# A causal mask as a fourth matmul pass, and a query rounding placed later on ScalarE and VectorE

## The chip, the cores and the metric

One core of a Trainium2 chip runs the whole program. The metric is the device time of one execution in microseconds (us). The kernel before takes 1631.67 us, the median of three runs.

## What is computed

A transformer layer: attention with a mixed key set, a residual and a layer norm, then a feed-forward part with Walsh-Hadamard transforms, a second residual and layer norm. Input is 4 x 1024 x 512 in float32. For the change only the attention's last 256 queries of each sequence matter. Cut to that:

```python
q_geo, k_geo = _rope(q_geo, pos, ROPE_BASE), _rope(k_geo, pos, ROPE_BASE)
remote = Tq - LW                     # 768; the first 768 keys are averaged in blocks of 64
pool = lambda a: concatenate([a[:, :, :remote].reshape(...).mean(axis=3), a[:, :, remote:]], axis=2)
k_pos = concatenate([arange(12) * 64 + 63, arange(768, 1024)])
scores = (q_sem @ k_sem2.T + q_geo @ k_geo2.T) / sqrt(32) * exp(logit_scale)
mask = k_pos[None, :] <= pos[:, None]
scores = where(mask, scores, -1e9)
probs = softmax(scores, axis=-1)
out = probs @ v2                     # 16 heads, 4 key heads
return out @ Wo
```

A query at position 768 or later sees all 12 averaged keys and the last 256 keys up to its own position. A query before 768 sees averaged keys only.

## The kernel before, in words

The program has two blocks, one after the other: `attention_block` (four sequences, called batches; the first three run in a hardware loop, the fourth stands behind it) and `ffn_block`, which the change leaves alone. Each engine runs its own instruction list in order, written out by hand, and waits on semaphores; a `Signal` counts how often a step has been done.

Precision is kept by splitting each float32 operand into a high part, rounded to `float32r`, and a low part, the rest. A product is three passes on TensorE (`three_passes`, lines 92 to 96): high x high, high x low, low x high. The rounding to the high part is ScalarE's (ACT), the subtraction that leaves the low part VectorE's (DVE) or GpSimd's (POOL).

A batch has 8 query tiles of 128 queries. Tiles 0 to 5 see averaged keys only. Tiles 6 and 7 (`tt` = 0 and 1) are the local ones: their scores have 12 + 128 = 140 and 12 + 256 = 268 keys. They are worked off in rounds. A group is one of the 4 key heads of one of the two tiles, so there are 8 groups (0 to 3 of the first tile, 4 to 7 of the second), with 4 query heads each, taken as two pairs. In round i of `ROUNDS` = 10:

- TensorE transposes the probabilities of group i-2 (`local_transposes`, L1098, into tile `mid`), makes the scores of group i (`local_scores`, L94 to L96 into `big`) and multiplies the transposed probabilities of group i-2 with the values (`local_values`, into `tr`). Between them stand the output products (`output`, into `acc`) and, in round 2, the transposes of the second tile's queries (`transpose_queries`, L929).
- VectorE adds the triangular mask to the last 128 keys of each pair of heads in PSUM (L800), takes the row maxima (L802), and later the reciprocals of the sums (L836). It makes low parts: of the transposed probabilities (`tp_lo`, L822), of the attended values (`qo_lo`, L848), and of the transposed queries (L790).
- ScalarE takes the exponentials with their sums (`local_exponentials`, L552), and makes high parts: `tp_hi` (L581), `qo_hi` (L601), and the queries' (`transposed_queries`, L508; the second tile's lie in the memory of `xs_hi` and `xs_lo`).
- GpSimd multiplies the exponentials by the reciprocals (`normalise`, L373 and L374).

The scores of a pair go into `pair_scores(tt, p)`: for the first tile into half a bank for each head (banks 0 and 1 in turn), for the second into a bank for each head (banks 2 and 3, then 0 and 1). So a pair's scores may start only when the exponentials of the pair two before have read theirs. The second tile's transposed queries lie in banks 2 and 3 until both parts are taken. The first scores of the second tile, in round 4, wait for the low part of those queries (`qt_lo_s`).

What TensorE does in round i, shortened:

```python
if i >= 2:
    local_transposes(i - 2)
if 1 <= i < GROUPS:
    local_scores(i)
if i == 2:
    transpose_queries(b, 1)
if i in (4, 8):
    output(b, RT + i // 8, 0)
if i >= 2:
    local_values(i - 2)
```

## Time and profile before

| what | value |
|---|---|
| three runs | 1630.94, 1631.67, 1631.96 us |
| the profiled execution's own time | 1631.06 us |
| its span, first to last instruction | 1628.9 us |
| mean granted TensorE clock, share of full | 0.982 |
| TensorE (PE) busy | 1544.5 us, 95% |
| TensorE weight loads (PEld) busy | 1382.1 us, 85% |
| VectorE (DVE) busy | 1065.5 us, 65% |
| ScalarE (ACT) busy | 617.8 us, 38% |
| GpSimd (POOL) busy | 464.1 us, 28% |

A TensorE row has two parts in this profile: the weight load (PEld) and the matmul (PE). Matmuls are pipelined: the duration of one holds its passage through the array, so what a pass costs is the distance from its start to the next one's. Idle time "before" an instruction is that of its engine, and the name behind the arrow is what released it.

### The profile page before, as it was taken

What the parts mean: (1) busy time and instruction counts of PE and PEld (TensorE: products, weight loads), DVE (VectorE), ACT (ScalarE), POOL (GpSimd) and SP (SyncE); (2) the same over time, 40 slices, a digit from 0 to 9 for tenths busy, and PEclk for the clock granted to TensorE, in tenths of its full rate; (3) what the DMA queues carried; (4) which work ended last, traced back from release to release, by engine and by line L of the source; (5) the groups of instructions that cost most, each with busy time, mean ns of one, the idle gap of its engine ahead of it and who ended that gap; (6) DMA issues with size and microseconds to landing.
All of it is one profiled execution on the core that took longest, in us unless ns stands there. A gap on an engine that the chain in (4) does not pass through costs nothing.

```text
span 1628.9 us, 28725 instructions
## 1 busy us (share of the span) xinstructions
PE 1544.5 (95%) x10152; PEld 1382.1 (85%) x10152; DVE 1065.5 (65%) x1835; ACT 617.8 (38%) x1255; POOL 464.1 (28%) x584
## 2 busy tenths in 40 slices
PE   6989999998998589999999999999999999999997
PEld 5976977887887478889999988999998999999996
DVE  6876777677687488885565565467556557557644
ACT  4253144236225344543343343333333333334322
POOL 5365356437346442330030030040021013003000
PEclk9999999999999889999999999999999999999999
DMA  6031122122211486677767756776867766866861
GB/s 264 17 111 51 33 78 97 35 78 98 68 65 40 167 324 258 246 277 249 263 221 262 272 205 226 277 236 230 309 200 243 280 235 219 287 234 223 284 230 64
DMA packets 92086, 307.72 MB, mean 189 GB/s; under 512 B 9888, under 2 KB 10272, under 8 KB 90144
## 3 DMA queue, kind: packets, MB, share of 16 engines
q1 hardware_dynamic: 90928, 301.54, 52.6%
q10 hardware_dynamic: 1008, 4.20, 0.6%
q8 instruction: 91, 1.49, 0.4%
q14 instruction: 59, 0.48, 0.1%
HBM read 255.37 MB, written 50.33 MB: 188 GB/s over the span
## 4 chain that ended last, share of the span: by engine, by line
PE 60%; DVE 3%; issue 1%; ACT 0%; POOL 0%; DVEq 0%; POOLq 0%; ACTq 0%
PE ff_bank_b L1747 16%; PE ff_bank_a L1747 10%; PE ff_bank_c L1747 10%; PE ff_acc L94 7%; PE ff_acc L96 7%; PE ff_acc L95 7%; DVE ff_d_lo L1561 1%; PE ff_x_ps L1718 1%; PE ff_x_ps L1700 1%; DVE ff_x_lo L1546 1%; DVE ff_ring L1551 0%; PE ff_x_ps L1708 0%; PE ff_x_ps L1709 0%; DVE ff_c L1607 0%; PE ff_acc L1797 0%
## 5 line engine op out<-in xcount | busy, mean ns | idle before, releaser
L1747 PE MATMUL ff_bank_b<-ff_x_hi,ff_ring 128*128 128x256 f32 x1536 | 306.4, 282 | 11.0 <-DVE ff_c L1601 8.0
L1747 PEld LDWEIGHTS ff_bank_b<-ff_x_hi,ff_ring 128*128 128x128 f32 x1536 | 250.7, 190 | 13.2 <-DVE ff_ring L1551 7.7
L1747 PE MATMUL ff_bank_b<-ff_x_lo,ff_ring 128*128 128x256 f32 x768 | 215.9, 281 | 0.0
L1747 PE MATMUL ff_bank_a<-ff_x_hi,ff_ring 128*128 128x256 f32 x1024 | 206.4, 284 | 7.9 <-issue 5.8
L94 PE MATMUL ff_acc<-ff_d_hi,ff_h_hi 128*128 128x512 f32 x512 | 203.8, 398 | 2.7 <-DVE ff_d_lo L1561 2.7
L1747 PE MATMUL ff_bank_c<-ff_x_hi,ff_ring 128*128 128x256 f32 x1024 | 204.9, 283 | 0.0
L96 PE MATMUL ff_acc<-ff_d_hi,ff_h_lo 128*128 128x512 f32 x512 | 199.7, 390 | 0.0
L95 PE MATMUL ff_acc<-ff_d_lo,ff_h_hi 128*128 128x512 f32 x512 | 199.4, 389 | 0.0
L1747 PEld LDWEIGHTS ff_bank_a<-ff_x_hi,ff_ring 128*128 128x128 f32 x1024 | 167.8, 191 | 11.8 <-issue 9.4
L1747 PEld LDWEIGHTS ff_bank_c<-ff_x_hi,ff_ring 128*128 128x128 f32 x1024 | 165.8, 188 | 1.9 <-issue 1.7
L1601 DVE TENSOR_TENSOR ff_c<-ff_bank_b,ff_c 128x512 f32<-128x512 f32 x64 | 44.2, 690 | 174.1 <-PE ff_bank_b L1747 168.9
L1747 PEld LDWEIGHTS ff_bank_b<-ff_x_lo,ff_ring 128*128 128x128 f32 x768 | 145.7, 190 | 0.0
L1747 PE MATMUL ff_bank_a<-ff_x_lo,ff_ring 128*128 128x256 f32 x512 | 144.2, 282 | 0.0
L1747 PE MATMUL ff_bank_c<-ff_x_lo,ff_ring 128*128 128x256 f32 x512 | 143.2, 280 | 0.0
L1452 ACT ACTIVATE ff_sg<-ff_c,h_ug_scale 128x512 f32<-128x512 f32 (+1 forms) x128 | 79.0, 617 | 136.8 <-DVE ff_c L1617 102.3
L94 PEld LDWEIGHTS ff_acc<-ff_d_hi,ff_h_hi 128*128 128x128 f32 x512 | 96.1, 188 | 23.0 <-issue 4.7
L1465 ACT ACTIVATE ff_c<-ff_bank_a 128x512 f32<-128x512 f32 x64 | 38.2, 597 | 202.6 <-PE ff_bank_a L1747 202.6
L96 PEld LDWEIGHTS ff_acc<-ff_d_hi,ff_h_lo 128*128 128x128 f32 x512 | 96.1, 188 | 21.2
L1637 DVE TENSOR_TENSOR ff_h_lo<-ff_hf,ff_h_hi 128x512 fp32r<-128x512 f32 x128 | 101.5, 830 | 18.0 <-ACT ff_h_hi L1494 17.4
L95 PEld LDWEIGHTS ff_acc<-ff_d_lo,ff_h_hi 128*128 128x128 f32 x512 | 96.2, 188 | 20.0 <-issue 1.7
L1747 PEld LDWEIGHTS ff_bank_a<-ff_x_lo,ff_ring 128*128 128x128 f32 x512 | 97.5, 190 | 2.6 <-issue 0.2
L1747 PEld LDWEIGHTS ff_bank_c<-ff_x_lo,ff_ring 128*128 128x128 f32 x512 | 96.2, 188 | 1.9 <-issue 1.9
(303 smaller groups left out, 3416.0 us busy)
## 6 DMA issues: line engine op xcount, KB each, us to landing
ff_ring<-gu_scratch SPq DMA_DIRECT2D x392, 512.0 KB, 4.9
gu_scratch<-ff_ring SPq DMA_DIRECT2D x56, 512.0 KB, 3.9
at_xt<-in_xt SPq DMA_DIRECT2D x4, 2048.0 KB, 8.3
at_xn<-in_x SPq DMA_DIRECT2D x32, 256.0 KB, 2.9
x_scratch<-at_x SPq DMA_DIRECT2D x32, 256.0 KB, 2.0
ff_raw<-in_wgu SPq DMA_DIRECT2D x8, 1024.0 KB, 6.4
at_wd_a<-in_wd SPq DMA_DIRECT2D x8, 512.0 KB, 3.8
mixed_scratch<-at_wd_a SPq DMA_DIRECT2D x8, 512.0 KB, 3.1
```

What stands on the lines that cost most here:

```text
L94: pe.matmul(out, lhs_hi, rhs_hi, start=first, stop=False)
L95: pe.matmul(out, lhs_hi, rhs_lo, start=False, stop=False)
L96: return pe.matmul(out, lhs_lo, rhs_hi, start=False, stop=last)
L1452: return act.activation(target, source, ACT.Silu, scale=ug_scale[:, 1, 2 * p + j:2 * p + j + 1])
L1465: act.activation(c2[:, 0, :, :], bank_a[:, :, :], ACT.Copy).then_inc(m1_s.sem, 1)
L1546: dve.tensor_tensor(x_lo[:, k, :, :], tokens(k), x_hi[:, k, :, :].bitcast(F32), ALU.subtract).then_inc(x_lo_s.sem, 1)
L1561: i = dve.tensor_tensor(by_piece(d_lo[:, j, :]), down_chunk(2 * p + j), by_piece(d_hi[:, j, :]).bitcast(F32), ALU.subtract)
L1601: dve.tensor_tensor(c12[:, :, :], bank_b[:, :, :], c2[:, 0, :, :], ALU.add).then_inc(evict_s.sem, 1)
L1637: dve.tensor_tensor(h_lo[q][:, 1 - j, :], hf[:, 1 - j, :], h_hi[q][:, 1 - j, :].bitcast(F32), ALU.subtract).then_inc(h_lo_s.sem, 1)
L1700: i = pe.transpose(x_ps[:, P * t:P * t + P], y[parity][:, t, P * c:P * c + P], ident[:, :])
L1718: pe.matmul(x_ps[:, :], had[:, :], down_chunk(i), start=True, stop=True).then_inc(w_had, 1)
L1747: i = pe.matmul(bank[:, m, :], r[:, a, m, c, :], b[:, k, c, :], start=(k < 3 and m == 0 and c == 0 and b is x_hi and a == 0), stop=(m == 1 ...
```

## The change

Two things. First, the addition of the mask in PSUM goes from VectorE, and its semaphore `lmasked` with it. In its place TensorE runs a fourth pass between the first and the second of each head's three: the identity (`ident_r`) as the stationary operand, the triangular mask (`causal_r`) as the moving one, 128 columns wide, accumulated into the last 128 keys. Both are `float32r` copies of tables that are in memory already, made once by ScalarE in the prologue. Second, the two parts of the second tile's transposed queries move on ScalarE and VectorE from round 2, behind that round's exponentials or reciprocals, to round 3, behind the transposed probabilities of group 1 and ahead of the maxima and exponentials of group 3.

```diff
@@ -188,6 +188,7 @@
         x1 = sb("x1", [P, 2, D])
         wd_a, wd_b = sb("wd_a", [P, IC, WC]), sb("wd_b", [P, IC, WC])
         bn, mv, rstd = sb("bn", [P, 2, 6]), sb("mv", [P, 2, 2]), sb("rstd", [P, 2, 2])
+        ident_r, causal_r = sb("ident_r", [P, P], F32R), sb("causal_r", [P, P], F32R)
 
         big = ps("big", [P, 4, 512])
         mid = ps("mid", [P, 2, 512])
@@ -209,6 +210,7 @@
         wq_hi_s, wq_lo_s, wo_hi_s, wo_lo_s = (sem(n) for n in ("wq_hi_s", "wq_lo_s", "wo_hi_s", "wo_lo_s"))
         wq_lo_pool = sem("wq_lo_pool")
         dve_past = pe_past = sem("past")
+        masks_s = sem("masks_s")
 
         xt_in = signal("xt_in", 16)
         xn_in = [signal(f"xn_in{i}", 16 * TILES // 2) for i in range(2)]
@@ -234,7 +236,7 @@
         qp_ps, qsem_s, lrope = signal("qp_ps", 2 * LT), signal("qsem_s", LT), signal("lrope", 6 * LT)
         lcopy = signal("lcopy", LT)
         qt_ps, qt_hi_s, qt_lo_s = signal("qt_ps", LT), signal("qt_hi_s", LT), signal("qt_lo_s", LT)
-        ls_ps, lmasked, lmax, lexp = signal("ls_ps", 8 * LT), signal("lmasked", 8 * LT), signal("lmax", 8 * LT), signal("lexp", 8 * LT)
+        ls_ps, lmax, lexp = signal("ls_ps", 8 * LT), signal("lmax", 8 * LT), signal("lexp", 8 * LT)
         lrecip, lnorm = signal("lrecip", 8 * LT), signal("lnorm", 8 * LT)
         NPT = [HKV * (tt + 1) for tt in range(LT)]
         tp_ps, tp_hi_s, tp_lo_s = signal("tp_ps", sum(NPT)), signal("tp_hi_s", sum(NPT)), signal("tp_lo_s", sum(NPT))
@@ -579,6 +581,8 @@
 
                             act.wait_ge(*(pv_ps.now(b, n - 1) if n >= 2 else vwo_ps.now(b, 2)))
                             act.activation(tp_hi[:, n % 2, :], mid[:, n % 2, :], ACT.Copy).then_inc(tp_hi_s.sem, 1)
+                    if i == 3:
+                        transposed_queries(b, 1)
                     if i in (5, 9):
                         pooled_hi(b, RT + i // 9)
                     if more and i == GROUPS:
@@ -586,8 +590,6 @@
                         split_x(b + 1, 1)
                     if 1 <= i < GROUPS:
                         local_exponentials(i)
-                    if i == 2:
-                        transposed_queries(b, 1)
                     if i in (3, 4):
                         scale_x1(b, RT - 5 + i)
                     if i == 7:
@@ -613,6 +615,9 @@
             for c in range(8):
                 act.wait_ge(wo_in[c], 16)
                 act.activation(wo_hi[:, c, :], wo_raw[c], ACT.Copy).then_inc(wo_hi_s, 1)
+            act.wait_ge(tab_in, 16 * 5)
+            act.activation(ident_r[:, :], ident[:, :], ACT.Copy).then_inc(masks_s, 1)
+            act.activation(causal_r[:, :], causal, ACT.Copy).then_inc(masks_s, 1)
             with act.Fori(0, B - 1) as b:
                 batch(b, True)
             batch(B - 1, False)
@@ -620,7 +625,7 @@
         @block.vector
         def _(dve):
             prime(dve, xsum, xpool_s, krope, v_lo_s, kr_s, kt_lo_s, bd_s, vbd_s, vb_lo_s, vwo_lo_s, qrope,
-                  masked, shifted, summed, probs_s, pt_lo_s, added, bn_s, qt_lo_s, lmasked, lmax,
+                  masked, shifted, summed, probs_s, pt_lo_s, added, bn_s, qt_lo_s, lmax,
                   lrecip, tp_lo_s, o_lo_s)
 
             dve.memset(pr[:, :, :, :], 0.0)
@@ -797,8 +802,6 @@
 
                         dve.wait_ge(*ls_ps.now(b, 8 * tt + p + 1))
                         pair = pair_scores(tt, p)
-                        dve.tensor_tensor(pair[:, :, keys - P:keys], pair[:, :, keys - P:keys], bc(causal, 1, 2), ALU.add).then_inc(lmasked.sem, 1)
-                        dve.wait_ge(*lmasked.now(b, 8 * tt + p + 1))
                         dve.tensor_reduce(stat[:, tt, 0, 2 * p:2 * p + 2], pair[:, :, 0:keys], AX.X, ALU.max, negate=True).then_inc(lmax.sem, 1)
 
                 for t in range(RT + 1):
@@ -820,6 +823,8 @@
                         for n in BLOCKS[i - 2]:
                             dve.wait_ge(*tp_hi_s.now(b, n + 1))
                             dve.tensor_tensor(tp_lo[:, n % 2, :], mid[:, n % 2, :], tp_hi[:, n % 2, :].bitcast(F32), ALU.subtract).then_inc(tp_lo_s.sem, 1)
+                    if i == 3:
+                        transposed_queries(1)
                     if i in (5, 9):
                         pooled_lo(b, RT + i // 9)
                     if more and i == GROUPS:
@@ -836,8 +841,6 @@
                             dve.reciprocal(stat[:, tt, 3, 2 * p:2 * p + 2], stat[:, tt, 1, 2 * p:2 * p + 2]).then_inc(lrecip.sem, 1)
                         if i == 1:
                             residual(b, RT - 1)
-                    if i == 2:
-                        transposed_queries(1)
                     if i == 6:
                         residual(b, TILES - 2)
                     if i >= 2:
@@ -1056,14 +1059,19 @@
                     tt, g = divmod(i, HKV)
                     keys = NB + P * (tt + 1)
                     pe.wait_ge(*qt_lo_s.now(b, tt + 1))
+                    pe.wait_ge(masks_s, 2)
                     for p in (2 * g, 2 * g + 1):
 
                         if tt or p >= 2:
                             pe.wait_ge(*lexp.now(b, 8 * tt + p - 1))
                         for h in (2 * p, 2 * p + 1):
                             a, s, j = h // 8, h // 4 % 2, h % 4
-                            i = three_passes(pe, pair_scores(tt, p)[:, h % 2, 0:keys], q_hi[tt][:, 4 * a + j, :], q_lo[tt][:, 4 * a + j, :],
-                                             kt_hi[:, a, s, 0:keys], kt_lo[:, a, s, 0:keys], True, True)
+                            out = pair_scores(tt, p)[:, h % 2, 0:keys]
+                            u, v = q_hi[tt][:, 4 * a + j, :], q_lo[tt][:, 4 * a + j, :]
+                            pe.matmul(out, u, kt_hi[:, a, s, 0:keys], start=True, stop=False)
+                            pe.matmul(out[:, keys - P:keys], ident_r[:, :], causal_r[:, :], start=False, stop=False, skip_group_check=True)
+                            pe.matmul(out, u, kt_lo[:, a, s, 0:keys], start=False, stop=False)
+                            i = pe.matmul(out, v, kt_hi[:, a, s, 0:keys], start=False, stop=True)
                         i.then_inc(ls_ps.sem, 1)
 
                 for t in range(RT + 1):
```

On TensorE, first round of the local scores, before (one head is three rows; `at_big` is the score tile, `at_kt_hi` and `at_kt_lo` the keys, `at_qo_hi` and `at_qo_lo` the first tile's queries):

```order
312 L95 MATMUL at_big<-at_kt_lo,at_qo_hi 128x140
313 L96 MATMUL at_big<-at_kt_hi,at_qo_lo 128x140
314 L94 MATMUL at_big<-at_kt_hi,at_qo_hi 128x140
315 L95 MATMUL at_big<-at_kt_lo,at_qo_hi 128x140
316 L96 MATMUL at_big<-at_kt_hi,at_qo_lo 128x140
```

and in the changed kernel:

```order
305 L1071 MATMUL at_big<-at_kt_hi,at_qo_hi 128x140
306 L1072 MATMUL at_big<-at_causal_r,at_ident_r 128x128
307 L1073 MATMUL at_big<-at_kt_lo,at_qo_hi 128x140
308 L1074 MATMUL at_big<-at_kt_hi,at_qo_lo 128x140
309 L1071 MATMUL at_big<-at_kt_hi,at_qo_hi 128x140
310 L1072 MATMUL at_big<-at_causal_r,at_ident_r 128x128
311 L1073 MATMUL at_big<-at_kt_lo,at_qo_hi 128x140
312 L1074 MATMUL at_big<-at_kt_hi,at_qo_lo 128x140
```

Behind each first pass stands one with the mask and the identity.

On VectorE, from the last maxima of round 2 to round 3, before (`at_stat` holds maxima and sums, `at_xs_lo<-at_big` is the second tile's queries, `at_qo_lo` here the attended values, `at_tp_lo` the transposed probabilities):

```order
214 L800 TENSOR_TENSOR at_big<-at_big,at_small 128x2x128
215 L802 TENSOR_REDUCE at_stat<-at_big 128x2
216 L836 RECIPROCAL at_stat<-at_stat 128x2 x2
217 L790 TENSOR_TENSOR at_xs_lo<-at_big,at_xs_hi 128x1024
218 L848 TENSOR_TENSOR at_qo_lo<-at_tr,at_qo_hi 64x512
219 L821 REGISTER_ALU
220 L822 TENSOR_TENSOR at_tp_lo<-at_mid,at_tp_hi 128x512
221 L800 TENSOR_TENSOR at_big<-at_big,at_small 128x2x128
222 L802 TENSOR_REDUCE at_stat<-at_big 128x2
```

and in the changed kernel:

```order
209 L805 TENSOR_REDUCE at_stat<-at_big 128x2
210 L841 RECIPROCAL at_stat<-at_stat 128x2 x2
211 L851 TENSOR_TENSOR at_qo_lo<-at_tr,at_qo_hi 64x512
212 L824 REGISTER_ALU
213 L825 TENSOR_TENSOR at_tp_lo<-at_mid,at_tp_hi 128x512
214 L795 TENSOR_TENSOR at_xs_lo<-at_big,at_xs_hi 128x1024
215 L805 TENSOR_REDUCE at_stat<-at_big 128x2
216 L803 REGISTER_ALU
217 L805 TENSOR_REDUCE at_stat<-at_big 128x2
```

The additions are gone, and the queries stand behind the two other low parts, directly ahead of the maxima of group 3.

On ScalarE at the same place, before (`128x140` are exponentials):

```order
87 L552 ACTIVATE at_union,at_stat<-at_big,at_stat 128x140 x2
88 L508 ACTIVATE at_xs_hi<-at_big 128x1024
89 L601 ACTIVATE at_qo_hi<-at_tr 64x512
90 L581 ACTIVATE at_tp_hi<-at_mid 128x512
91 L548 REGISTER_ALU
92 L552 ACTIVATE at_union,at_stat<-at_big,at_stat 128x140 x4
```

and in the changed kernel:

```order
89 L554 ACTIVATE at_union,at_stat<-at_big,at_stat 128x140 x2
90 L603 ACTIVATE at_qo_hi<-at_tr 64x512
91 L583 ACTIVATE at_tp_hi<-at_mid 128x512
92 L510 ACTIVATE at_xs_hi<-at_big 128x1024
93 L550 REGISTER_ALU
94 L554 ACTIVATE at_union,at_stat<-at_big,at_stat 128x140 x4
```

The queries' high part went from the first to the third place between the two groups' exponentials.

## Rows read from the trace of the kernel before

**Rows 1.** Page, span and part 1: engine, busy us (share), instructions.

```profile
span 1628.9 us, 28725 instructions
...
PE 1544.5 (95%) x10152; PEld 1382.1 (85%) x10152; DVE 1065.5 (65%) x1835; ACT 617.8 (38%) x1255; POOL 464.1 (28%) x584
```

**Rows 2.** Busy time by stretch: length, engines, PEclk, DMA share, GB/s.

```profile
82.00:215.00 133.00, 125.84 (x757) 104.52 (x756) 93.15 (x196) 49.81 (x131) 64.77 (x102) 0.97 0.19 65
...
109.00:110.00 1.00, 1.00 (x7) 0.80 (x5) 0.55 (x2) 1.00 (x6) 0.30 (x2) 0.50 0.00 0
```

**Rows 3.** TensorE's weight loads, 82 to 152 us: waited for, us, times, longest.

```profile
PEld at_tr L94 <- DVE at_tp_lo L822: 4.4, 4, 2.6
...
PEld at_big L94 <- ACT at_union L552: 1.7, 5, 0.9
PEld at_mid L1098 <- POOL at_union L374: 1.1, 2, 0.6
```

**Rows 4.** Groups by form, attention: count, busy us, mean ns, idle before.

```profile
L552 ACT ACTIVATE at_union<-at_big,at_stat 128x268 f32<-128x268 f32 x64 | 30.4, 479 | 35.0 <-DVE at_stat L802 32.4 <-PE at_mid L1098 2.1
...
L800 DVE TENSOR_TENSOR at_big<-at_big,at_small 128x256 f32<-128x256 f32 x64 | 26.9, 421 | 3.9 <-PE at_big L96 3.9
```

**Rows 5.** TensorE in order of time: start us, us, operation, count.

```profile
116.61 0.37 PE L94 MATMUL at_big<-at_kt_hi,at_xs_hi 128*128 128x268 f32 x1
116.81 0.29 PE L95 MATMUL at_big<-at_kt_lo,at_xs_hi 128*128 128x268 f32 x1
116.94 0.29 PE L96 MATMUL at_big<-at_kt_hi,at_xs_lo 128*128 128x268 f32 x1
...
210.47 1.03 PE L1051 MATMUL at_mid<-at_kg_bd,at_union 128*128 128x96 f32 x8
```

**Rows 6.** VectorE in order of time, first local round.

```profile
93.16 0.45 DVE L802 TENSOR_REDUCE at_stat<-at_big 128x2 f32<-128x280 f32 x1
93.53 0.42 DVE L800 TENSOR_TENSOR at_big<-at_big,at_small 128x256 f32<-128x256 f32 x1
93.98 0.45 DVE L802 TENSOR_REDUCE at_stat<-at_big 128x2 f32<-128x280 f32 x1
```

**Rows 7.** ScalarE in order of time, end of round 2 and round 3.

```profile
104.28 1.02 ACT L508 ACTIVATE at_xs_hi<-at_big 128x1024 fp32r<-128x1024 f32 x1
105.18 0.58 ACT L601 ACTIVATE at_qo_hi<-at_tr 64x512 fp32r<-64x512 f32 x1
105.66 0.59 ACT L581 ACTIVATE at_tp_hi<-at_mid 128x512 fp32r<-128x512 f32 x1
108.60 0.38 ACT L552 ACTIVATE at_union<-at_big,at_stat 128x140 f32<-128x140 f32 x1 [2.36 <-DVE at_stat L802]
...
110.14 0.81 ACT L486 ACTIVATE at_x<-at_x,at_rstd 128x512 f32<-128x512 f32 x1
```

**Rows 8.** VectorE in order of time, same place.

```profile
105.33 1.23 DVE L790 TENSOR_TENSOR at_xs_lo<-at_big,at_xs_hi 128x1024 fp32r<-128x1024 f32 x1 [0.75 <-ACT at_xs_hi L508]
106.47 0.67 DVE L848 TENSOR_TENSOR at_qo_lo<-at_tr,at_qo_hi 64x512 fp32r<-64x512 f32 x1
107.07 0.67 DVE L822 TENSOR_TENSOR at_tp_lo<-at_mid,at_tp_hi 128x512 fp32r<-128x512 f32 x1
```

**Rows 9.** TensorE in order of time: after its longest waits, and round 8's keys.

```profile
107.80 0.79 PE L94 MATMUL at_tr<-at_tp_hi,at_v_hi 128*128 128x512 f32 x1 [2.47 <-DVE at_tp_lo L822]
...
112.44 0.47 PE L94 MATMUL at_acc<-at_wo_hi,at_qo_hi 128*128 128x512 f32 x1 [0.37 <-DVE at_qo_lo L848]
...
134.20 3.70 PE L961 MATMUL at_big<-at_wkv,at_xt 128*128 128x512 f32 x8 [0.22 <-ACT at_union L552]
```

**Rows 10.** TensorE in order of time, last batch, round 8.

```profile
532.85 0.47 PE L94 MATMUL at_acc<-at_wo_hi,at_qo_hi 128*128 128x512 f32 x1 [3.39 <-DVE at_qo_lo L848]
...
533.39 0.40 PE L96 MATMUL at_acc<-at_wo_hi,at_qo_lo 128*128 128x512 f32 x1
...
534.53 0.63 PE L94 MATMUL at_acc<-at_wo_hi,at_qo_hi 128*128 128x512 f32 x1
```

## The prediction

> **What bounds the kernel now.** I read the page's totals first, then the stretches by batch, then TensorE's waits, then the order of time in one batch's local rounds. TensorE is busy for 1544.5 us of a span of 1628.9 us [rows 1], so anything that only relieves another engine pays through TensorE's waits and nowhere else. The change touches the attention part alone, about the first third of the span. There a loop batch takes 133 us, TensorE busy in 126 of it [rows 2]. The weight-load rows show its waits more sharply, as a matmul's row carries its drain: in one batch's local stretch 4.4 us for the rounded-off part of the transposed probabilities, 1.7 us for exponentials on ScalarE and 1.1 us for GpSimd [rows 3]. So 7.2 us a batch, some 29 us over four, is all that a quicker VectorE or ScalarE could ever give back, beside one long wait at the end of the last batch (below). The reader should see in [rows 4] that 64 mask additions cost VectorE 26.9 us, and that ScalarE is idle for 32.4 us before the second tile's exponentials because the row maxima come late.
>
> **Part 1, added passes.** Each of 16 heads x 2 tiles x 4 batches gets a 128-column pass: 128 passes. No such pass with these operands is in the trace. The nearest is the 96-column pass that also lands in a part of a running accumulation: eight of them last 1.03 us; less one pass's own length of 0.29, that is 0.74/7 = 0.106 us each [rows 5]; a 268-column score pass takes 0.13 us from start to start (116.81 to 116.94) [rows 5]. I take 0.11 us: 3.5 us a batch, 14.1 us in all, 0.44 us in each of eight rounds. Bounds: 0.106 below and 0.20 above (the spacing behind the first score pass after other work, 116.61 to 116.81, if each mask pass were paid like that) [rows 5], which is 25.6 us in all. The Trainium skill ("TensorE: Matmul & The Clock Gate", section "Back-to-back issue gap") states about 81 ns for 128 columns with their own weight load. By that the passes would cost 10.4 us and the total would come out up to 3.7 us lower; the rows here show 0.106 for fewer columns, and the measurement decides.
>
> **Part 2, removed additions.** An addition starts 0.45 us before its reduction (93.53 to 93.98), and the reduction holds VectorE for 0.37 us until the next addition [rows 6]. Per pair 0.45 us goes, 7.2 us a batch. Of a round's two, only the first is on the path to the exponentials: the second lies beside ScalarE's work on the first pair. The second half of the round's gain is slack on VectorE.
>
> **Part 3, the moved rounding.** In round 2 ScalarE rounds the second tile's queries at 104.28, then the first attended values at 105.18, then the second group's transposed probabilities at 105.66 [rows 7]. VectorE follows with the queries' low part at 105.33, then 106.47 and 107.07 [rows 8]. TensorE has been idle for 2.47 us when it starts the second group's values at 107.80 [rows 9]. This is the largest wait of the batch. Now the queries come last of the three.
> - Exponentials of group 2 end at 104.28 before. They end about 0.65 us earlier: 0.45 for the addition just ahead of them and 0.2 gained in the rounds before, where VectorE was late. So 103.63.
> - ScalarE: values rounded from 103.63, probabilities from 104.11, queries from about 104.65 (steps 0.48 and 0.5 as in [rows 7]).
> - VectorE: 0.6 after ScalarE's start (such a rounding takes 0.58 there [rows 7]), 104.26, then 0.60 for the next [rows 8], 104.86. TensorE starts the values 0.73 after that, as now (107.07 to 107.80): 105.6, which is 2.2 us earlier.
> - The queries' low part starts 1.05 after ScalarE's (104.28 to 105.33), so 105.70, and takes 1.14 (105.33 to 106.47). The group-3 maxima start at 106.84, the exponentials 0.45 later: 107.3 against 108.60 [rows 7]. **Here 0.9 of the 2.2 is given back**: the queries' rounding is now ahead of the maxima, and TensorE's first second-tile scores wait for those exponentials instead.
> - ScalarE's next scaling and the output matmuls follow the exponentials: 110.14 and 112.44 [rows 7, 9] become 108.85 and 111.15. Round 4 is left 1.3 us early. The two extra passes per pair fit into TensorE's wait ahead of it (its scores run from about 108.25 to 110.2, output starts 111.15).
>
> **Part 4, rounds 5 to 7.** TensorE gets 3 x 0.44 = 1.3 us more. Of its waits, those of [rows 3] less the one of 2.6 leave 1.8 + 1.7 + 1.1 = 4.6 us; half of them, 2.3, I put in these rounds, up to the next batch's keys at 134.20, where it waits for exponentials still [rows 9]. The exponentials move forward by more than 2 us in these rounds, because their maxima lose an addition each round and ScalarE was waiting for them [rows 4]; I count about 2.1 of these 2.3 as gone. So 2.1 - 1.3 = 0.8 more: **2.1 us per loop batch**. From there TensorE runs without a wait over keys and output, so the gain stays.
>
> **Part 5, last batch.** There no keys of a next batch fill round 8. TensorE waits 3.39 us until 532.85 [rows 10] for a chain that runs through the last exponentials, ScalarE's rounding of the attended values and VectorE's low part of them. This chain gains the 2.1 and the last round's addition, less half a score pass: 2.7 us.
>
> **Clock.** After the 2.47 us idle the granted clock stands at 0.50 of full, so at 1.2 GHz [rows 2]. It costs nothing now, since the output at 112.44 waits for ScalarE anyway; if it falls a little later instead, it could cost up to 1.5 us a batch. In the last batch a 512-column pass some time after the 3.39 us idle lasts 0.63 us (534.53) against 0.40 a little earlier (533.39) [rows 10]; about eight passes stand there, 0.2 longer each, 1.6 us. I keep both as they are. A mean clock of 0.97 over a batch of 133 us [rows 2] is some 8 us at half clock, so another such stretch lies elsewhere in the batch, worth up to 1.5 us, and a shift of 2 us can take it away or bring one more.
>
> **At nothing:** two small copies on ScalarE in the prologue (below 0.4 us each by the shortest rows of [rows 7]), behind the same engine's rounding of the output weights and beside TensorE's own first projections; if that cover were gone, 0.7 us. No DMA is added. The semaphore wait for the tables is met once and for all.
>
> **Sum.** 3 x 2.1 + 2.7 = 9.0 us. The profiled execution took 1631.06 us around its span of 1628.9, so 1622.1; the median shown is 0.6 above it, and with half of that I say 1622.4. A measurement of this kernel can tell about 0.2%, 3.3 us, from no change.
>
> **Rivals.**
> - *The wait moves, it does not go* (chance 0.12): the queries' low part, now late, and the exponentials behind it hold round 4 at the old 112.44. Then only Part 4 and the last batch pay, 0.8 x 3 + 1.4 = 3.8: about 1627.3. For it: the rounding takes 1.14 us on VectorE and stands directly ahead of the maxima. Against: even so I find the exponentials 1.3 us earlier than 108.60.
> - *More than forecast* (0.13): the shorter idle times keep the clock at 2.4 GHz in the last batch and in a loop batch or two: another 1.6 + 2 us, about 1618.8.
> - *TensorE is the bound and pays* (0.06, slower): all 14.1 us of passes lie on its path, and the exponentials, released 0.45 us earlier, find ScalarE or GpSimd behind, so that the second half gains nothing. The move alone gives 4 x 2.2 = 8.8. So +5.3, about 1636.4. It decides if a pass costs more than 7.2/32 = 0.22 us, or if the waits filled in a batch stay below the 3.5 us of passes. Against it: GpSimd waits for VectorE before each pair from round 3 on, and the waits listed are larger.
> - *The change does not do what it says* (0.02): the pass is absorbed elsewhere and nothing moves, 1631.
>
> **Numbers.** The forecast has 0.67. The range reaches from the clock's case to the moved wait: 1617.5 to 1627.5. Faster by over 0.2%: the forecast, the clock's case and most of the moved wait, 0.87; same 0.08; slower 0.05.
>
> **What would show it.** VectorE's rows lose 64 additions of 0.42 us; 128 passes of about 0.11 us appear; TensorE's wait for the low part of the transposed probabilities falls from 4.4 to about 1.5 us a batch, and a new wait of 1 to 1.5 us stands before the first second-tile scores; a loop batch takes about 131 us. A pass spacing over 0.15, or output matmuls of round 4 no earlier than before, would make it wrong.

## The result and the profile after

The changed kernel took 1613.55 us (median of four, 1612.44 to 1616.1) against 1631.31 for the kernel before (median of four, 1627.54 to 1631.96): ratio 0.9903, interval 0.9891 to 0.9916. A second set of the same comparison (below) gave 1618.41 against 1629.46, ratio 0.9923, 0.9904 to 0.9942. So the gain is 11 to 18 us, where 9.0 was forecast. The first set's time lies below the stated range of 1617.5 to 1627.5, the second set's just inside it. Ratios leave out two executions far outside their fellows (1922 us of the kernel without mask passes, 6093 us of the kernel before). The page of the changed kernel, against [rows 1]:

```profile
span 1611.5 us, 28943 instructions
...
PE 1540.3 (96%) x10280; PEld 1385.8 (86%) x10280; DVE 1039.5 (65%) x1771; ACT 616.2 (38%) x1257; POOL 463.7 (29%) x584
```

TensorE has 128 instructions more and VectorE 64 fewer. The mask passes and the exponentials, by form (against [rows 4]):

```profile
L1072 PE MATMUL at_big<-at_causal_r,at_ident_r 128*128 128x128 f32 x128 | 31.4, 245 | 0.0
L554 ACT ACTIVATE at_union<-at_big,at_stat 128x268 f32<-128x268 f32 x64 | 30.1, 482 | 25.2 <-DVE at_stat L805 25.2
```

A mask pass never waits. ScalarE's idle time for the second tile's maxima fell from 32.4 to 25.2 us. TensorE's weight-load waits from 82 to 152 us, the first batch (against [rows 3]):

```profile
PEld at_big L1071 <- ACT at_union L554: 1.4, 1, 1.4
PEld at_mid L1106 <- POOL at_union L376: 1.0, 1, 1.0
...
PEld at_acc L94 <- DVE at_qo_lo L851: 0.4, 1, 0.4
PEld at_tr L94 <- DVE at_tp_lo L825: 0.3, 1, 0.3
```

The largest before, 4.4 us for the low part of the transposed probabilities, is down to 0.3. The exponentials' wait is now a single one of 1.4 us, ahead of the first scores of round 4. The 0.4 for attended values stands at 150.6 us, behind the local rounds. ScalarE, VectorE and TensorE in order of time (against [rows 7], [rows 8] and [rows 9]):

```profile
102.65 0.38 ACT L552 ACTIVATE at_union<-at_big,at_stat 128x140 f32<-128x140 f32 x1 [3.50 <-DVE at_stat L802]
...
103.55 0.38 ACT L552 ACTIVATE at_union<-at_big,at_stat 128x140 f32<-128x140 f32 x1
```

(ScalarE before: the first exponential of each pair of group 2) and in the changed kernel:

```profile
100.93 0.38 ACT L554 ACTIVATE at_union<-at_big,at_stat 128x140 f32<-128x140 f32 x1 [2.36 <-DVE at_stat L805]
...
101.65 0.37 ACT L554 ACTIVATE at_union<-at_big,at_stat 128x140 f32<-128x140 f32 x1
...
102.36 0.59 ACT L603 ACTIVATE at_qo_hi<-at_tr 64x512 fp32r<-64x512 f32 x1
102.83 0.59 ACT L583 ACTIVATE at_tp_hi<-at_mid 128x512 fp32r<-128x512 f32 x1
103.31 1.03 ACT L510 ACTIVATE at_xs_hi<-at_big 128x1024 fp32r<-128x1024 f32 x1
105.98 0.38 ACT L554 ACTIVATE at_union<-at_big,at_stat 128x140 f32<-128x140 f32 x1 [1.65 <-DVE at_stat L805]
```

```profile
102.98 0.68 DVE L851 TENSOR_TENSOR at_qo_lo<-at_tr,at_qo_hi 64x512 fp32r<-64x512 f32 x1 [0.30 <-ACT at_qo_hi L603]
103.59 0.67 DVE L825 TENSOR_TENSOR at_tp_lo<-at_mid,at_tp_hi 128x512 fp32r<-128x512 f32 x1
104.37 1.22 DVE L795 TENSOR_TENSOR at_xs_lo<-at_big,at_xs_hi 128x1024 fp32r<-128x1024 f32 x1
105.51 0.80 DVE L805 TENSOR_REDUCE at_stat<-at_big 128x2 f32<-128x280 f32 x2
```

```profile
86.85 1.03 PE L932 MATMUL at_big<-h_ident,at_qrot 128*128 128x128 f32 x8
...
104.36 0.46 PE L94 MATMUL at_tr<-at_tp_hi,at_v_hi 128*128 128x512 f32 x1
...
109.72 0.47 PE L94 MATMUL at_acc<-at_wo_hi,at_qo_hi 128*128 128x512 f32 x1 [0.67 <-DVE at_qo_lo L851]
...
130.13 2.31 PE L964 MATMUL at_big<-at_wkv,at_xt 128*128 128x512 f32 x5
```

L932 is the transposes of the first tile's queries, which stand at 87.76 in the trace before. From here on I measure a batch's **local stretch**, from those transposes to the next batch's keys (L961 before, L964 now): it leaves out whatever happened earlier in the execution. It went from 134.20 - 87.76 = 46.4 us to 130.13 - 86.85 = 43.3, by 3.2 us (46.44 less 43.28). The same number comes out in all three loop batches of either trace, to 0.1 us. The last batch has no next keys; there I take the output products of round 8. Inside it:

| from the query transposes to | before | after | gain | forecast |
|---|---|---|---|---|
| values of group 1 (counting from 0), round 3 | 20.0 | 17.5 | 2.5 | 2.2 |
| output products, round 4 | 24.7 | 22.9 | 1.8 | 1.3 |
| next batch's keys, round 8 | 46.4 | 43.3 | 3.2 | 2.1 |
| output products of round 8, last batch | 49.5 | 46.0 | 3.5 | 2.7 |

Three times 3.16 and 3.5 make 13.0 us. The two profiled executions differ by 17.4 us of span. Of the rest, 0.9 us was there before the first local round (86.85 against 87.76), and 3.2 us is the granted clock, twice 1.6 us, in two places where the change does nothing: in the trace before, TensorE ran at 1.2 GHz behind the small matmuls of the second and third batch, in the one after it did not. Some 0.3 us stays unassigned. The feed-forward part, from TensorE's first matmul of it to the end, took 1074.3 us before and 1074.7 after.

### The profile page after: what moved, and what is told of

The parts are those of the page before. It is cut to its first block, busy times and chain, and to the rows that moved or that the text cites. A ratio compares the mean times of both kernels' runs of the same rounds, so it can differ in the third digit from the quotient of the medians.

```text
span 1611.5 us, 28943 instructions
## 1 busy us (share of the span) xinstructions
PE 1540.3 (96%) x10280; PEld 1385.8 (86%) x10280; DVE 1039.5 (65%) x1771; ACT 616.2 (38%) x1257; POOL 463.7 (29%) x584
## 4 chain that ended last, share of the span: by engine, by line
PE 60%; DVE 4%; issue 2%; ACT 0%; POOL 0%; DVEq 0%; POOLq 0%; ACTq 0%
PE ff_bank_b L1755 16%; PE ff_bank_a L1755 10%; PE ff_bank_c L1755 10%; PE ff_acc L94 7%; PE ff_acc L96 7%; PE ff_acc L95 7%; DVE ff_d_lo L1569 1%; PE ff_x_ps L1726 1%; PE ff_x_ps L1708 1%; DVE ff_x_lo L1554 1%; DVE ff_ring L1559 0%; PE ff_x_ps L1716 0%; PE ff_x_ps L1717 0%; DVE ff_c L1615 0%; DVE ff_bn L1691 0%
## 5 line engine op out<-in xcount | busy, mean ns | idle before, releaser
L1609 DVE TENSOR_TENSOR ff_c<-ff_bank_b,ff_c 128x512 f32<-128x512 f32 x64 | 44.2, 690 | 173.6 <-PE ff_bank_b L1755 173.6
L94 PEld LDWEIGHTS ff_acc<-ff_d_hi,ff_h_hi 128*128 128x128 f32 x512 | 96.1, 188 | 22.9 <-issue 4.7
L1645 DVE TENSOR_TENSOR ff_h_lo<-ff_hf,ff_h_hi 128x512 fp32r<-128x512 f32 x128 | 100.4, 822 | 18.0 <-ACT ff_h_hi L1502 17.4
L1358 POOL TENSOR_TENSOR ff_xm<-ff_xm 128x512 f32<-128x512 f32 x7 | 9.0, 1288 | 311.1 <-ACT ff_xm L1430 311.1
```

The lines of the kernel that those rows point to most:

```text
L94: pe.matmul(out, lhs_hi, rhs_hi, start=first, stop=False)
L1609: dve.tensor_tensor(c12[:, :, :], bank_b[:, :, :], c2[:, 0, :, :], ALU.add).then_inc(evict_s.sem, 1)
L1645: dve.tensor_tensor(h_lo[q][:, 1 - j, :], hf[:, 1 - j, :], h_hi[q][:, 1 - j, :].bitcast(F32), ALU.subtract).then_inc(h_lo_s.sem, 1)
```

## The experiments

**Each part alone, the passes removed, the passes doubled.** Edits, the first against the changed kernel, the second against the one before, the others against the changed one:

```diff
 # e1_mask_only: transposed_queries back in round 2, on ACT and VectorE
-                    if i == 3:
+                    if i == 2:
                         transposed_queries(b, 1)
```
```diff
 # e2_move_only: the VectorE mask stays, only the rounding moves
-                    if i == 2:
+                    if i == 3:
                         transposed_queries(b, 1)
```
```diff
 # e3_no_mask_moved (e4_mask_twice has the line twice)
-                            pe.matmul(out[:, keys - P:keys], ident_r[:, :], causal_r[:, :], start=False, stop=False, ...)
```

In the first two, both lines also change places within the round, on ScalarE and on VectorE: behind the exponentials or reciprocals in round 2, ahead of the maxima and exponentials in round 3. The third kernel leaves the causal mask of the local scores out altogether.

> The mask pass alone: TensorE adds the mask, the second tile's queries are still rounded in round 2. Theory A (both parts matter about alike in the local rounds, each some 1.5 us a batch, and they add): 1624 to 1627 us. Theory B (the mask additions on VectorE were the main delay, 0.45 us before every pair's exponentials plus 0.2 between the pairs): 1617 to 1621. Theory C (the moved rounding does it, the mask pass pays for itself): 1629 to 1633. In the trace TensorE's wait before the second group's values stays at about 2 us.

> The moved rounding alone: VectorE still adds the mask. Theory A: 1624 to 1627 us, TensorE's wait before the second group's values falls from 2.6 to about 0.6 us and a wait of 1 to 2 us for exponentials appears in round 4. Theory B: 1628 to 1631. Theory C: 1615 to 1619.

> The changed kernel without its mask passes, so the local scores are not masked at all: what 128 passes of 0.11 us (14.1 us) cost in place. Theory A (passes of rounds 1 to 4 stand beside waits, those of rounds 5 to 7 are paid): 1.3 to 2 us a batch, 1606 to 1609 us. Theory B (TensorE sets the pace throughout): the whole 14 us, 1600 us.

> The changed kernel with each mask pass issued twice (masked scores get -2e9 in place of -1e9). Theory A: the second pass costs like the first or somewhat more, since the waits are smaller now: 1.5 to 2.7 us a batch, 1619 to 1625 us. Theory B (TensorE sets the pace throughout): 1627 to 1628.

Measured against 1629.25 us for the kernel before: the mask pass alone 1616.79 (ratio 0.9924, 0.9899 to 0.9949), the move alone 1629.78 (0.9997, 0.9985 to 1.001), without passes 1606.6 (0.986, 0.9838 to 0.9881), passes doubled 1619.8 (0.9941, 0.992 to 0.9961). The first two say theory B (1616.79 against its 1617 to 1621, 1629.78 against its 1628 to 1631): **the gain is the mask's, the move alone gives nothing in the times that can be told from zero.** The trace of the move alone shows why. TensorE with the move alone:

```profile
106.58 0.50 PE L94 MATMUL at_tr<-at_tp_hi,at_v_hi 128*128 128x512 f32 x1 [0.90 <-DVE at_tp_lo L822]
109.60 0.39 PE L94 MATMUL at_big<-at_kt_hi,at_xs_hi 128*128 128x268 f32 x1 [1.61 <-ACT at_union L552]
112.56 0.48 PE L94 MATMUL at_acc<-at_wo_hi,at_qo_hi 128*128 128x512 f32 x1 [1.13 <-DVE at_qo_lo L848]
```

and VectorE:

```profile
105.25 0.68 DVE L848 TENSOR_TENSOR at_qo_lo<-at_tr,at_qo_hi 64x512 fp32r<-64x512 f32 x1 [0.31 <-ACT at_qo_hi L601]
105.86 0.67 DVE L822 TENSOR_TENSOR at_tp_lo<-at_mid,at_tp_hi 128x512 fp32r<-128x512 f32 x1
106.64 1.23 DVE L790 TENSOR_TENSOR at_xs_lo<-at_big,at_xs_hi 128x1024 fp32r<-128x1024 f32 x1
107.78 0.42 DVE L800 TENSOR_TENSOR at_big<-at_big,at_small 128x256 f32<-128x256 f32 x1
```

The wait of 2.47 us [rows 9] fell to 0.90, and in its place stand 1.61 us for exponentials and 1.13 for attended values. The mask addition of group 3 starts at 107.78, 19.7 us after the query transposes of this trace (88.10); in the kernel before, behind the same three low parts in another order, it started at 107.67, which is 19.9 us after them. The three have to be done before the maxima in either order, so the exponentials do not come earlier. The local stretch of this kernel is 46.2 us, against 46.4.

With the mask pass alone it is 43.5 us in the second batch and 44.1 and 44.2 in the first and third; in the fourth, round 4's output starts as early as in the second (23.1 us, against 23.8). In the first and third the clock fell behind the wait that is still there. The first and the second batch:

```profile
106.87 0.50 PE L94 MATMUL at_tr<-at_tp_hi,at_v_hi 128*128 128x512 f32 x1 [1.36 <-DVE at_tp_lo L825]
...
235.44 0.50 PE L94 MATMUL at_tr<-at_tp_hi,at_v_hi 128*128 128x512 f32 x1 [1.36 <-DVE at_tp_lo L825]
239.51 0.47 PE L94 MATMUL at_acc<-at_wo_hi,at_qo_hi 128*128 128x512 f32 x1 [0.67 <-DVE at_qo_lo L851]
```

```profile
109.00:110.00 1.00, 1.00 (x6) 1.00 (x6) 0.00 (x0) 0.98 (x2) 0.86 (x3) 0.50 0.06 16
237.00:238.00 1.00, 1.00 (x11) 1.00 (x10) 0.17 (x1) 1.00 (x3) 1.00 (x4) 1.00 0.00 0
```

(busy time by stretch, as in [rows 2]: a mean clock of 0.50 after the same wait of 1.36 us in the first batch, 1.00 in the second). So beside the mask the move is worth 0.2 to 0.3 us a batch at full clock, and another 0.6 in those batches in which it keeps the clock from falling.

The passes' own price: without them the stretch is 42.1 us, with each twice 45.4. So 32 passes cost 1.2 us of the 3.5 they take, and 32 more cost 2.1. Both times lie in the ranges of theory A (1606 to 1609 and 1619 to 1625), the 1.2 us a little under its 1.3 to 2. But theory A's place for the price holds only in part: without the passes round 4's output starts 0.5 us earlier (22.4 us after the query transposes, against 22.9), so 0.5 of the 1.2 is paid until there and 0.7 behind it. Since the kernel with the move alone (46.2 us) and the one without passes (42.1) differ by the additions only, all additions together cost 4.1 us a batch.

**The clock in the long waits, the two pairs apart, and ScalarE's scaling.**

```diff
 # e5_before_filled, against the kernel before; keep_busy issues n matmuls into at_acc
+                    if i == 3:
+                        keep_busy(b, RT - 1, 8)
+                    if i == 8 and not more:
+                        keep_busy(b, TILES - 1, 11)
```
```diff
 # e6_vector_second, against the changed kernel (e7_vector_first: 1 and 0 changed over)
+                        if p % 2 == 1:
+                            dve.tensor_tensor(pair[:, :, keys - P:keys], ..., bc(causal, 1, 2), ALU.add).then_inc(lmasked.sem, 1)
+                            dve.wait_ge(*lmasked.now(b, 4 * tt + p // 2 + 1))
...
+                            if p % 2 == 0:
+                                pe.matmul(out[:, keys - P:keys], ident_r[:, :], causal_r[:, :], ...)
```
```diff
 # e8_scale_late, against the changed kernel: these lines move behind the qo_hi rounding of the round
                     if i in (3, 4):
                         scale_x1(b, RT - 5 + i)
                     if i == 7:
                         scale_x1(b, TILES - 2)
```

In the two kernels with a pair on each engine the copies of the tables are also counted on another semaphore (`wo_hi_s` in place of `masks_s`); the work is the same.

> The kernel before with matmuls on TensorE whose results nobody reads: 8 passes of 512 columns (1.9 us) in its wait of round 3, 11 in the wait of round 8 of the last batch, so that it is not idle there; all other work is the same. Theory A (a good part of the gain is the granted clock, which fell after these waits): the clock stays at full there, 0.5 to 1 us less a batch and 1.5 at the end, 1624 to 1627 us beside 1629 to 1631. Theory B (the low clock after those waits stood beside other waits and cost only 1.5 us in the last batch): 1627.5 to 1629.5.

> The changed kernel, but only the first pair of each group is masked by TensorE, the second by VectorE as before. Theory A (as in the prediction, the second addition of a round stands beside ScalarE's work on the first pair): no later exponentials, and 64 passes fewer, so 1609 to 1612 us. Theory B (the second addition delays the second pair's exponentials by 0.2 us or more a round, and with them everything behind them on ScalarE): 1613 to 1617.

> The changed kernel, but VectorE masks the first pair of each group and TensorE the second. Theory A and B alike: the first addition delays both pairs, 0.45 us a round in the rounds that wait for exponentials, 1615 to 1620 us; if the two pairs counted alike it would equal the run with the second pair.

> The changed kernel with ScalarE's scaling of the normalised rows in rounds 3, 4 and 7 placed behind the rounding of the attended values instead of ahead of it. TensorE waits 0.7 us for those values before round 4's output products and 2.4 us in the last batch. If these waits are on the path: 0.7 us a batch and 0.8 in the last, 1609 to 1611 us. If GpSimd or the exponentials stand behind them at once: 1612 to 1614.

Measured against 1629.33: filled 1629.7 (0.9999, 0.9984 to 1.0014), VectorE for the second pair 1613.84 (0.9909, 0.9885 to 0.9934), for the first pair 1620.76 (0.9949, 0.9932 to 0.9967), scaling late 1611.54 (0.9902, 0.9872 to 0.9932).

The filled kernel:

```profile
105.08 2.05 PE L1104 MATMUL at_acc<-at_wo_hi 128*128 128x512 f32 x8
107.72 0.50 PE L94 MATMUL at_tr<-at_tp_hi,at_v_hi 128*128 128x512 f32 x1 [0.58 <-DVE at_tp_lo L822]
...
112.36 0.48 PE L94 MATMUL at_acc<-at_wo_hi,at_qo_hi 128*128 128x512 f32 x1 [1.13 <-DVE at_qo_lo L848]
```

```profile
109.00:110.00 1.00, 0.73 (x6) 0.60 (x5) 0.48 (x2) 1.00 (x6) 0.37 (x2) 1.00 0.00 0
```

The clock stays at full, the scores are done sooner, and TensorE then waits 1.13 us instead of 0.37 [rows 9] for the same attended values. The output starts 24.7 us after the query transposes, as before, and the local stretch is 46.4 us, as before. So in the kernel before the change, the low clock behind that wait cost nothing, as the prediction had it, and it is not where the gain comes from.

The last batch is another matter. There round 8's output starts at the same time after the query transposes (49.5 us), but the passes behind it stay at full clock:

```profile
528.64 0.48 PE L94 MATMUL at_acc<-at_wo_hi,at_qo_hi 128*128 128x512 f32 x1 [0.86 <-DVE at_qo_lo L848]
...
535.16 0.40 PE L895 MATMUL at_mid<-h_ident,at_pr 128*104 128x128 f32 x2 [1.22 <-DVE at_tp_lo L822]
```

From that output to the transposes of L895 it is 6.5 us, against 8.1 in the kernel before (532.85 to 540.93), where the clock fell behind 3.39 us of idle. So there the low clock cost 1.6 us, once in an execution, the prediction's number. Theory B said both, with 1627.5 to 1629.5 for the time; the median of 1629.7 lies just above, and an interval of over 2 us to either side cannot show the 1.6.

The pairs: with VectorE masking the second pair the local stretch is 43.5 us, the first 45.2. Already the first number is above the changed kernel's 43.3, with 16 passes fewer a batch; were the second additions free, it would be below. I estimate the 16 passes at 0.6, half of the 1.2 of the run without passes. Then the eight second additions of a batch cost about 0.2 + 0.6 = 0.8 us and the eight first ones 1.9 + 0.6 = 2.5. These sum to 3.3, not to the 4.1 of all additions: both together cost 0.8 us more than the sum of each alone. The second addition is not free: theory B (1613.84 in its 1613 to 1617), though the time comes out even with the changed kernel's, since the saved passes pay for it. The first pair's 1620.76 lies just above its expected 1615 to 1620, and the two pairs do not count alike.

The late scaling starts round 4's output 0.7 us earlier (22.2 after the query transposes), but the next keys by less than 0.1 us. Only the last batch keeps it, 45.2 against 46.0. The median of 1611.54 lies between what the two cases had said, 2 us under the changed kernel's of the first set, and the interval covers that one's ratio.

**Again, and two further orders.**

```diff
 # e11_queries_last, against the changed kernel, VectorE (e12_all_moves adds e8's edit and this one on GpSimd)
-                    if i == 3:
-                        transposed_queries(1)
...
                         if i:
                             local_maxima(i)
+                        if i == 3:
+                            transposed_queries(1)
```
```diff
 # e12_all_moves, GpSimd
-                        if tt == 0 and p in (1, 3):
-                            inverse_deviation(b, RT - 2 + p // 3)
+                        if tt == 0 and p in (3, 5):
+                            inverse_deviation(b, RT - 2 + p // 5)
```

> The changed kernel once more, for its spread and for another trace: 1612 to 1617 us. If the gain in the local rounds does not hang on the granted clock, each batch takes 43.3 us again from its first query transposes to the next batch's keys, whatever the clock does elsewhere; if it does, some batches are longer by 0.7 us or more.

> The kernel before once more, for another trace: 46.4 us a batch in the same stretch. If the two spells of low clock at the small matmuls of the second and third batch are a matter of where they fall, they stand elsewhere or are missing here, and the time differs by about 1.6 us for each; if they belong to this kernel, they are there again.

> The changed kernel, with VectorE's low part of the second tile's queries behind round 3's maxima instead of ahead of them. Theory A (moving the rounding from round 2 to 3 gave almost nothing because it stands ahead of the same maxima in both places): now the exponentials of group 3 come 1.1 us earlier, the first second-tile scores about 0.5 us; output of round 4 0.5 to 1.1 us earlier, and 0 to 0.7 us a batch in the end, 1610.5 to 1613.5. Theory B (the queries' low part itself holds TensorE): scores of round 4 0.8 us later, 1614 to 1617.

> The run before, with ScalarE's scaling behind the rounding of the attended values and GpSimd's inverse deviations of two tiles each one step later, so that the second group is normalised first. Each wait of TensorE that was left (1.0 for GpSimd, 1.4 for exponentials, 0.7 for attended values) should shrink. If TensorE is the bound behind round 4: 1 to 1.8 us a batch less than the changed kernel, 1606 to 1610 us; if the exponentials are, 1610 to 1612.

Measured against 1629.46: the changed kernel 1618.41 (0.9923, 0.9904 to 0.9942), the one before 1629.29 (one execution), queries last 1611.03 (0.9881, 0.9851 to 0.9911), all moves 1609.74 (0.9867, 0.9848 to 0.9886). The changed kernel was above its expected range of 1612 to 1617, and yet its local stretches were 43.3 us in each loop batch and 46.0 in the last, exactly as in the first trace. What was longer is elsewhere. Behind the small matmuls of the first and second batch:

```profile
45.82 2.00 PE L1027 MATMUL at_mid<-at_ks_bd,at_wqs 128*128 128x48 f32 x16
47.60 0.73 PE L94 MATMUL at_acc<-at_wo_hi,at_tp_hi 128*104 128x512 f32 x1
48.13 0.63 PE L95 MATMUL at_acc<-at_wo_lo,at_tp_hi 128*104 128x512 f32 x1
```

```profile
48.00:50.00 2.00, 2.00 (x6) 1.32 (x6) 1.97 (x3) 0.67 (x1) 2.00 (x2) 0.50 0.00 0
```

The clock is 0.50 there, in a kernel whose first trace showed 1.00 at the same place, and the stretch from the first of these matmuls to the scores of the averaged keys (L1047) is 1.6 us longer for it (10.6 against 9.1). The kernel before, run again, has this in its first batch and not in the second and third; its local stretches are 46.5 us, as before. And the feed-forward part, which no kernel here touches, took 1071.7 to 1078.6 us over the fourteen traces, and 1078.2 in this one against 1074.7 in the first, the largest single piece of the difference. In the last batch it is the other way round. Behind a wait as long as in the first trace (2.38 us there, shown below) the clock stayed at full:

```profile
519.04 0.47 PE L94 MATMUL at_acc<-at_wo_hi,at_qo_hi 128*128 128x512 f32 x1 [2.39 <-DVE at_qo_lo L851]
519.35 0.40 PE L95 MATMUL at_acc<-at_wo_lo,at_qo_hi 128*128 128x512 f32 x1
...
525.57 0.40 PE L898 MATMUL at_mid<-h_ident,at_pr 128*104 128x128 f32 x2 [1.22 <-DVE at_tp_lo L825]
```

From that output to the transposes of L898 it took 6.5 us, against 8.1 in the first trace. So spells of low clock come and go between executions of one kernel, and the 3.2 us of the first comparison cannot be credited to the change. One thing stays open: why the four executions of the changed kernel in the first set were shorter, but for one of 1616.1 us, than those of the second (1616.08 to 1619.63).

The queries last, VectorE and TensorE:

```profile
103.85 0.67 DVE L825 TENSOR_TENSOR at_tp_lo<-at_mid,at_tp_hi 128x512 fp32r<-128x512 f32 x1
104.45 0.82 DVE L805 TENSOR_REDUCE at_stat<-at_big 128x2 f32<-128x280 f32 x2
105.19 1.22 DVE L795 TENSOR_TENSOR at_xs_lo<-at_big,at_xs_hi 128x1024 fp32r<-128x1024 f32 x1
```

```profile
106.53 0.39 PE L1071 MATMUL at_big<-at_kt_hi,at_xs_hi 128*128 128x268 f32 x1 [0.55 <-ACT at_union L554]
108.66 0.47 PE L94 MATMUL at_acc<-at_wo_hi,at_qo_hi 128*128 128x512 f32 x1
```

The wait before the second tile's scores is down from 1.15 to 0.55 us (from 1.4 to 0.8 in the rows of weight loads), the output of round 4 starts without one, 21.5 us after the query transposes instead of 22.9, and the stretch is 42.0 us: **1.3 us a batch from setting the rounding behind the maxima**, five to six times what setting it behind the probabilities gave. It is the test of the reading above, and theory A of that run holds (1611.03 in its 1610.5 to 1613.5), with more than the 0 to 0.7 us that it expected at the end of the stretch. With all moves the loop stretches are 42.4 us, 0.4 longer, and the last batch's 44.2 (against 44.7); the wait of 1.0 us for GpSimd is gone from the list, 1.1 us for the low part of the transposed probabilities stand there instead of 0.3, and the loop batches gained nothing by it: 0.9 us a batch less than the changed kernel, where 1 to 1.8 was expected. Both versions' medians lie below the changed kernel's 1618.41 in the same set, and all of the last one's executions (1606.38 to 1610.13) below all of the changed kernel's.

## Why the prediction was wrong

The sign, the engine and the order of size were right; the sum of 9.0 us should have been 13.0 by the local stretches. The medians stand on either side of that, 17.8 us in the first set and 11.1 in the second, by what differs elsewhere between executions. **The step that failed is "only the first is on the path" in Part 2, which put the second addition of a round at nothing; it costs about 0.8 us a batch. With it goes the term of Part 4 that halved the remaining waits.** Per loop batch 1.1 us is missing from the forecast: 0.5 until round 4's output, 0.6 behind it. Point by point:

- **What bounds the kernel** held. TensorE's waits were what could be filled, and the 7.2 us a batch of [rows 3] fell to 2.7 of the same kinds, in spite of 3.5 us of new passes.
- **Part 1, the passes.** Taken at 0.11 us. The trace has a head's four passes in 0.48 us (126.93 to 127.41 in the changed kernel), of which three took 0.37 before (117.06 to 117.43): 0.11. What they cost on the path is 1.2 us a batch by the run without them, where 1.3 was put. The size is right, the place not quite: the prediction had it all in rounds 5 to 7, the run has 0.5 of it ahead of round 4's output.
- **Part 2, the removed additions, is where it failed.** "Of a round's two, only the first is on the path ... the second lies beside ScalarE's work" is false: the runs with one pair on VectorE give the second additions about 0.8 us a batch, some 0.6 of it until round 4's output (23.2 us after the query transposes with the second pair on VectorE, 22.9 in the changed kernel, and an estimated 0.2 for the passes left out). In group 2 the four exponentials took 1.63 us before (102.65 to 104.28) and 1.43 now (100.93 to 102.36), 0.2 us less: the second pair started 0.90 us after the first before (103.55) and 0.72 now (101.65), because its maximum was late by that much after the first pair's exponentials. I had compared VectorE's 0.82 us a pair with nothing; ScalarE needs 0.72 for two exponentials of 140 keys. With it the end of group 2's exponentials is 1.0 us earlier and not 0.65 (counted from the query transposes), and group 3's 1.7 and not 1.3.
- **Part 3, the moved rounding**, got its first number nearly right (values 2.5 us earlier, 2.2 forecast) and credited it wrongly. It said that 0.9 of 2.2 is given back and 1.3 stays by the move. By the run with the move alone, the values start 1.55 us earlier (18.5 us after the query transposes, against 20.0) and all but 0.2 is given back. The 1.3 (1.8 measured, 1.55 of it with the mask alone) is the additions' again: one ahead of group 2's exponentials, one ahead of group 3's, and the gaps between pairs. The arithmetic had both in it, and I read the sum as the move's. What I did not ask is whether the work ahead of the maxima becomes less; it is the same three low parts in both orders.
- **Part 4, rounds 5 to 7**: 0.8 forecast, 1.4 measured (21.8 to 20.4 us from round 4's output to the keys). I had put half of the remaining waits in these rounds, 2.3 us, an assumed half, and counted 2.1 of them as gone. The trace before has 2.7 there (its weight-load waits from 118.82 to the keys at 134.20: 0.7 and 0.3 for transposed probabilities, 0.9, 0.3 and 0.5 for exponentials), and in the changed kernel none of these is left: 2.7 less 1.3 for the passes is the 1.4. With the second pair on VectorE this part gained no more for its fewer passes (20.3 us), so about half of the missing 0.6 is the second additions' again. That split rests on the estimate for the passes.
- **Part 5, the last batch**: 2.7 forecast, 3.5 measured, the size following from the same terms. In the second trace the clock does not fall behind that wait (above), in the first it still does, after 2.38 us of idle:

```profile
515.15 0.53 PE L94 MATMUL at_acc<-at_wo_hi,at_qo_hi 128*128 128x512 f32 x1 [2.38 <-DVE at_qo_lo L851]
515.48 0.63 PE L95 MATMUL at_acc<-at_wo_lo,at_qo_hi 128*128 128x512 f32 x1
```

- **The clock.** "It costs nothing now" in round 3 was right, by the filled kernel. That it could cost if it fell later was right, by the mask alone (0.6 us in two of its batches). In the last batch it cost the forecast 1.6 us, by the filled kernel. That spells elsewhere can be missing or more is what the traces show, 3.2 us between the first two; that a shift by the change does it is not shown, since they differ between two executions of one kernel as well.
- **Rivals.** "The wait moves, it does not go" is exactly what the moved rounding does by itself. "More than forecast" came nearest, and that its 1618.8 agrees with the second set's 1618.41 is luck: it had the excess from the clock, and the excess of 13.0 over 9.0 lies in the local stretches at full clock. Only its last-batch part was seen, 1.5 us in the second trace. "TensorE is the bound and pays" fails by the passes' 1.2 us. The range was drawn from the clock at its lower end and had no room for a gain larger than forecast in the mask itself.
- **What would show it**: the wait for the transposed probabilities' low part fell to 0.3 and not 1.5 us; the new wait before the second tile's scores is 1.4, as forecast.

## What to carry to other kernels

When an instruction is moved in an engine's queue, count what stands ahead of each thing that others wait for, before and after: a wait is only gained for the ones that it now stands behind. Moved but still ahead of the same maxima, this rounding took 1.6 us off TensorE's largest wait and gave 0.2 us a batch; its VectorE part behind the maxima gave 1.3. When two pieces of work alternate between two engines, compare the period of both (0.82 us a pair on VectorE, 0.72 on ScalarE) before calling the second piece hidden. And measure such a change by a stretch that starts and ends at the same instructions in both traces: it repeated to 0.1 us in every kernel here but one (the mask alone, 0.6 us, where the clock fell inside it), while whole executions of the changed kernel spread over 7 us.

## What the runs showed of the hardware

- A float32r pass of 128 columns into part of a running accumulation is spaced much like the other score passes: 0.11 us, against 0.12 for 268 columns. The Trainium skill ("TensorE: Matmul & The Clock Gate", section "Back-to-back issue gap") has about 81 ns for 128 columns; this kernel's rows do not show it.
- The length of a wait did not decide whether the granted clock fell behind it. After one and the same wait of 1.36 us it fell to 0.50 in one batch and stayed at 1.00 in the next, in one trace. After 2.38 us it fell in the changed kernel's first trace and after 2.39 us it stayed in its second. With the first pair on VectorE it stayed after 3.15 us of the last batch:

```profile
526.16 0.47 PE L94 MATMUL at_acc<-at_wo_hi,at_qo_hi 128*128 128x512 f32 x1 [3.15 <-DVE at_qo_lo L854]
526.47 0.39 PE L95 MATMUL at_acc<-at_wo_lo,at_qo_hi 128*128 128x512 f32 x1
```

- It also fell behind 32 passes of 48 columns that left TensorE busy throughout, in some executions and batches and not in others, at 1.6 us each.
- Keeping the clock up bought nothing where another wait followed (round 3, the same 46.4 us a batch), and 1.6 us where the passes behind it were on the path (round 8 of the last batch).
